# Two layers of a transformer on one core: attention's matrix order from a list schedule, its projections reordered

## What is computed

```
xn  = layernorm(x)                              # per token, no gain
q, k, v = split(xn @ w_qkv); 16 heads of 16     # 2 batches, 2048 tokens
q, k = rope(q), rope(k)
att = softmax(causal(q k^T / 4)); o = att @ v
x1  = x + o @ w_out + ffn(xn)                   # 256 -> 1024 -> 256, signed weights, gelu
```

## Time and profile before

| | us |
|---|---|
| profiled execution | 1663.91 |
| its span, first to last instruction | 1662.0 |
| projections, 0 to the first attention matmul | 148.7 |
| attention, 148.7 to the last copy | 871.3 |
| everything after | 642.0 |
| TensorE busy, share of the span | 1316.7, 79% |
| VectorE | 1271.5, 77% |
| ScalarE | 987.9, 59% |
| GpSimd | 319.4, 19% |

### The profile page before, as it was taken

The page is one execution under the profiler, slowest core; times in us unless marked ns, Lnnn a source line. Parts: engine busy times, 40 slices in busy tenths (PEclk is TensorE's granted clock), DMA queues, the critical chain, the costliest instruction groups (busy, mean ns, idle before and its releaser), DMA issues. The chain is left out here.

```text
span 1662.0 us, 27637 instructions
## 1 busy us (share of the span) xinstructions
PE 1316.7 (79%) x9558; PEld 588.4 (35%) x9558; DVE 1271.5 (77%) x1880; ACT 987.9 (59%) x1292; POOL 319.4 (19%) x574
## 2 busy tenths in 40 slices
PE   4783788888888888888888987888727876679987
PEld 2442222222222222222222222566523343358754
DVE  6984887988779787798897951478758999575668
ACT  3541355777768777677786886556417646236642
POOL 2210000110101101011010110322100047600365
PEclk9896577999889998899998998899967988789999
DMA  7875302140321403204032022656644134576767
GB/s 219 277 228 149 65 8 41 18 91 9 76 41 19 92 7 75 42 17 91 10 74 42 8 44 61 182 178 199 201 162 138 61 127 155 182 229 203 236 194 237
DMA packets 159723, 186.24 MB, mean 112 GB/s; under 512 B 19556, under 2 KB 135652, under 8 KB 158564
## 3 DMA queue, kind: packets, MB, share of 16 engines
q1 hardware_dynamic: 153448, 167.78, 35.9%
q0 software_dynamic: 6144, 16.79, 3.1%
HBM read 100.88 MB, written 83.36 MB: 111 GB/s over the span
## 5 line engine op out<-in xcount | busy, mean ns | idle before, releaser
L1270 ACT ACTIVATE att_prob<-att_score,late_score_scale 128x1024 f32<-128x1024 f32 (+3 forms) x640 | 594.7, 988 | 271.4 <-PE att_score L1359 269.3
L1241 DVE TENSOR_REDUCE att_m_part<-att_mx 128x2 f32<-128x1024 f32 (+3 forms) x408 | 473.3, 1160 | 97.5 <-PE att_mx L1308 43.6
L1343 PE MATMUL att_pv<-att_prob,early_v 128*32 128x512 f32 (+3 forms) x2560 | 324.5, 581 | 0.5 <-POOL att_prob L1206 0.2
L1302 PE MATMUL att_mx<-early_kop,early_qop 48*128 48x512 f16 (+3 forms) x944 | 181.1, 367 | 118.0 <-DVE att_m_part L1241 106.2
L1359 PE MATMUL att_score<-early_qop,early_kop 50*128 50x512 f16 (+3 forms) x1280 | 261.0, 369 | 12.4 <-ACT att_prob L1270 5.9
L1206 POOL TENSOR_SCALAR_AFFINE_SELECT att_prob<-att_prob 128x256 f32<-128x256 f32 x256 | 103.1, 407 | 767.6 <-ACT att_prob L1270 767.4
L1241 DVE TENSOR_REDUCE att_m_part<-att_mx_one 128x1 f32<-128x384 f32 (+1 forms) x336 | 220.9, 657 | 37.4 <-PE att_mx_one L1302 32.1
L1359 PEld LDWEIGHTS att_score<-early_qop,early_kop 50*128 50x128 f16 x1280 | 69.5, 95 | 293.5 <-ACT att_prob L1270 188.7
L1302 PE MATMUL att_mx_one<-early_kop,early_qop 48*128 48x384 f16 (+1 forms) x336 | 134.1, 399 | 19.7 <-DVE att_m_part L1241 15.9
L2108 PE MATMUL rwkv_prod<-rwkv_xm,late_mixT 128*128 128x512 f32 x192 | 100.1, 677 | 29.1 <-DVE rwkv_xm L1978 16.6
L1302 PEld LDWEIGHTS att_mx<-early_kop,early_qop 48*128 48x128 f16 x944 | 51.7, 97 | 190.9 <-DVE att_m_part L1241 165.9
(11 more groups left out here) (259 smaller groups left out, 1901.2 us busy)
## 6 DMA issues: line engine op xcount, KB each, us to landing
moe_xt<-rows SPq DMA_DIRECT2D x46, 256.0 KB, 3.3
results<-moe_y SPq DMA_DIRECT2D x46, 256.0 KB, 2.6
qk<-qkv_parts SPq DMA_DIRECT2D x32, 256.0 KB, 3.6
va<-qkv_v SPq DMA_DIRECT2D x8, 1024.0 KB, 6.5
early_v<-va SPq DMA_DIRECT2D x8, 1024.0 KB, 5.2
routing_xp<-parts SPq DMA_DIRECT2D x32, 256.0 KB, 3.7
rows<-att_zeros SPq DMA_DIRECT2D x8, 864.0 KB, 6.2
early_kop<-qk SPq DMA_DIRECT2D x48, 128.0 KB, 4.5
```

Source lines behind the costliest of these rows:

```text
L1241: nc.vector.tensor_reduce(cells[:, sides[0]:sides[-1] + 1, some], bank.rearrange("p a (h w) -> p a h w", w=w), AX.X, ALU.max).then_inc(m_f ...
L1270: nc.scalar.activation(prob[:, r % (PROBS * HP), :, n0:], score[:, r % 2, :, n0:], ACT.Exp, scale=late_weights.score_scale[:, 0:1])\
L1302: op = nc.tensor.matmul(bank[a][:, n * w:(n + 1) * w], qop[rows, slot, t, hp, i * P:(i + 1) * P], kop[rows, slot, hp, c * GT:c * GT + w], ...
L1343: op = nc.tensor.matmul(pv[at, n0:], v[:, slot, j, at], prob[:, (st * HP + h // 2) % (PROBS * HP), h % 2, n0:], start=(j == 0), stop=(j == ...
```

## The change

In the projections, from the second group on, `low` moves ahead of `products` on VectorE, `high` ahead of the late weight copies and `first_part` on ScalarE, and `ln.turn` ahead of `heads` on TensorE. The query loads of several blocks go in one DMA per head pair, part and side: 12 where 18 (or, for a whole head group, 24) were, and the semaphore targets follow; the first maxima of block 1 wait for all 12, those of block 2 for the values only.

In attention `spread_entries`, `spots` and `BEHIND` go. `matrix_order` writes one order over all head groups at build time. It keeps a clock for each engine and planned durations, and at each turn takes the maximum entry, score or value product that can start first; of equals the maximum first, then the score. The order of entries among themselves, of scores and of value products stays, as do their sizes and banks. ScalarE's exponentials and copies are taken from the same list: a copy stands where the list has the block's last value product. VectorE and GpSimd are unrolled.

```diff
     HP = HG // 2
     QB, KB = T // GT, T // P
     LOADS = 6
-    FIRST, REST = 16 * 2 * LOADS, 16 * (LOADS * (QB - 1) + 1)
+    FIRST, SECOND, REST = 16 * (LOADS + HP * LOADS), 16 * HP * LOADS, 16
 
     def __init__(self, s):
         self.qop = s.sb("qop", [P, 2, self.QB, self.HP, GT], F16)
@@ -643,12 +643,18 @@
                           qk_d[1, bass.ds(hg * (HG * D), HG * D), part, bass.ds(b * T, T)]
                           .rearrange("(hp a d) t -> a d hp t", a=2, d=D)[a]).then_inc(self.first_in[slot], 16)
 
-    def load_q(self, eng, qk_d, b, hg, slot, t, signal):
+    def load_q(self, eng, qk_d, b, hg, slot, blocks, signal):
+        n = blocks.stop - blocks.start
+        toks = bass.ds(b * T + blocks.start * GT, n * GT)
         for a, row, (_, part) in self.blocks:
             at = self.HALF * a + row * D
-            eng.dma_start(self.qop[at:at + D, slot, t],
-                          qk_d[0, bass.ds(hg * (HG * D), HG * D), part, bass.ds(b * T + t * GT, GT)]
-                          .rearrange("(hp a d) t -> a d hp t", a=2, d=D)[a]).then_inc(signal, 16)
+            src = qk_d[0, bass.ds(hg * (HG * D), HG * D), part, toks].rearrange("(hp a d) t -> a hp d t", a=2, d=D)[a]
+            if n == 1:
+                eng.dma_start(self.qop[at:at + D, slot, blocks.start], src.rearrange("hp d t -> d hp t")).then_inc(signal, 16)
+                continue
+            for hp in range(self.HP):
+                eng.dma_start(self.qop[at:at + D, slot, blocks, hp], src[hp].rearrange("d (q t) -> d q t", t=GT))\
+                    .then_inc(signal, 16)
 
     def load_v(self, eng, va_d, b, hg, slot):
         eng.dma_start(self.v[:, slot].rearrange("p j n -> p (j n)"),
@@ -769,12 +775,11 @@
                     if at[3][0] == G - 2:
...
                         att_in.load_k(sp, qk_d, 0, 0, 0)
-                        att_in.load_q(sp, qk_d, 0, 0, 0, 0, att_in.first_in[0])
+                        att_in.load_q(sp, qk_d, 0, 0, 0, slice(0, 1), att_in.first_in[0])
...
-            for t in range(1, att_in.QB):
-                att_in.load_q(sp, qk_d, 0, 0, 0, t, att_in.second_in if t == 1 else att_in.rest_in[0])
-            sp.sem_inc(att_in.rest_in[0], 16 * att_in.LOADS)
+            att_in.load_q(sp, qk_d, 0, 0, 0, slice(1, att_in.QB), att_in.second_in)
+            sp.sem_inc(att_in.first_in[0], att_in.FIRST - 16 * 2 * att_in.LOADS)
...
+                early = mid and mid[0] == 0
+                if new and not early:
+                    low(*new)
                 for p in range(QK):
                     if mid:
                         products(*mid, p)
                         rotated(*mid, p)
-                if new:
+                if new and early:
                     low(*new)
...
+                if new and not early:
+                    high(*new)
                 if mid and mid[0] >= late_from:
                     for n in late_turns(mid[0]):
                         late_weights.copy(nc, act, n, late_banks)
                 if mid:
                     first_part(*mid, 0)
-                if new:
+                if new and early:
                     high(*new)
...
+                if new and not early:
+                    ln.turn(nc, pe, new[0], new[1], ident[:, :])
                 if mid:
-                    if not mid[0]:
+                    if early:
                         pe.wait_ge(w.found, w.ready)
                     pe.wait_ge(ln.lo_done.sem, ln.lo_done.done(mid[0]))
                     heads(*mid, 0)
                     if mid[0] >= late_from:
                         late(mid[0])
                     heads(*mid, 1)
-                if new:
+                if new and early:
                     ln.turn(nc, pe, new[0], new[1], ident[:, :])
...
+    entries = [(0, e) for e in early if e != ("turn", LATE)]
+    for it in range(NIT):
+        entries += [(it, e) for e in late]
+        entries += [(it, e) if e == ("turn", LATE) else (it + 1, e) for e in early if it + 1 < NIT or e == ("turn", LATE)]
+    place = {entry: k for k, entry in enumerate(entries)}
+
+    def banks_of(k):
+        e = entries[k][1]
+        return (0, 1) if e[0] == "max" and len(e[5]) == 2 else (2,)
+    used, before = {}, []
+    for k in range(len(entries)):
+        before.append(max((used.get(bank, -1) for bank in banks_of(k)), default=-1))
+        used.update({bank: k for bank in banks_of(k)})
+
+    def columns(t, j):
+        return GT - max(0, j - TG * t) * P
+
+    def matrix_order():
+
+
+        hand, back, mask, row, copy = 250, 120, 420, 6500, 580
+        turn = {"max": 0, "score": 1, "value": 2}
+        score_at = [(it, st, hp) for it in range(NIT) for st in range(NS) for hp in range(HP)]
+        value_at = [(it, st) for it in range(NIT) for st in range(NS)]
+        pe = dve = act = pool = 0
+        exp_end, prob_end, value_end, out_end, found, rows = [], [], [], [], {}, {}
+        bank_end, order, done = [0] * BANKS, [], {"max": 0, "score": 0, "value": 0}
+        total = {"max": len(entries), "score": len(score_at), "value": len(value_at)}
+        while done != total:
+            ready = []
+            n = done["max"]
+            if n < total["max"]:
+                it, e = entries[n]
+                need = [bank_end[bank] for bank in banks_of(n)] + ([found[it, e[1]]] if e[0] == "turn" else [])
+                ready.append((max(need) + back, "max"))
+            n = done["score"]
+            if n < total["score"]:
+                it, st, hp = score_at[n]
+                if (it, steps[st][0]) in rows and n // HP < done["value"] + PROBS:
+                    need = [rows[it, steps[st][0]]] + [end + back for end in exp_end[n - 2:n - 1] if n >= 2]
+                    ready.append((max(need), "score"))
+            n = done["value"]
+            if (n + 1) * HP <= done["score"]:
+                need = prob_end[n * HP:(n + 1) * HP] + (out_end[-1:] if steps[n % NS][1] == 0 else [])
+                ready.append((max(need) + back, "value"))
+            when, kind = min((max(pe, when), turn[kind], kind) for when, kind in ready)[::2]
+            n = done[kind]
+            done[kind] += 1
+            if kind == "max":
+                it, e = entries[n]
+                if e[0] == "turn":
+                    pe = when + 270
+                    dve = max(dve, pe + hand) + 700
+                    rows[it, e[1]] = dve + row
+                else:
+                    size = len(e[3]) * width(e[1], e[2], e[4])
+                    pe = when + 20 + size * 5 // 12 + (60 * len(e[3]) if e[4] == e[1] else 0)
+                    dve = max(dve, pe + hand) + 70 + size * len(e[5]) * 100 // 96
+                    if e == chunks(e[1])[-1]:
+                        dve += 400
+                        found[it, e[1]] = dve
+                for bank in banks_of(n):
+                    bank_end[bank] = dve
+                order.append((kind, n))
+                continue
+            it, st = (score_at if kind == "score" else value_at)[n][:2]
+            t, j = steps[st]
+            if kind == "score":
+                pe = when + 20 + columns(t, j) * 5 // 12
+                start = max([act, pe + hand] + value_end[it * NS + st - PROBS:it * NS + st - PROBS + 1]
+                            if it * NS + st >= PROBS else [act, pe + hand])
+                act = start + 30 + columns(t, j) * 2 * 100 // 96
+                exp_end.append(act)
+                pool = max(pool, act + 100) + mask if j >= TG * t else pool
+                prob_end.append(pool if j >= TG * t else act)
+            else:
+                pe = when + 150 + columns(t, j) * 5 // 3
+                value_end.append(pe + hand)
+                if st in last_step:
+                    act = max(act, pe + hand) + copy
+                    out_end.append(act)
+            order.append((kind, it, st) + ((score_at[n][2],) if kind == "score" else ()))
+        return order
+
+    order = matrix_order()
...
+                att_in.load_q(sp, qk_d, b, hg, slot, slice(0, QB), first_in[slot])
...
+            for k, (it, e) in enumerate(entries):
+                entry(k, it, e)
...
+            for kind, it, st, *hp in [at for at in order if at[0] != "max"]:
+                if kind == "score":
+                    exps(it, st, *hp)
+                elif st in last_step:
+                    copy_out(it, steps[st][0])
...
+                if it > 0 and e == chunks(0)[0]:
+                    pe.wait_ge(first_in[slot], (it // 2 + 1) * FIRST)
+                    pe.wait_ge(rest_in[slot], (it // 2 + 1) * REST)
+                if it == 0 and e == chunks(1)[0]:
+                    pe.wait_ge(second_in, att_in.SECOND)
+                if it == 0 and e == chunks(2)[0]:
+                    pe.wait_ge(rest_in[0], REST)
+                if before[k] >= 0:
+                    pe.wait_ge(m_found, before[k] + 1)
...
+            for kind, *at in order:
+                if kind == "max":
+                    entry(*at)
```

(4 more changed lines are left out.)

227 lines of the change are left out of this document (64 added, 163 removed).

## The result

The changed kernel takes **1685.2 us** (median of four runs, 1683.4 to 1686.6) against 1665.1 for the kernel before in the same comparison (1660.1 to 1671.0): a ratio of **1.012 [1.010, 1.015]**, slower by a little over 1%. The prediction had 1605 us and faster. The profiled execution spans 1681.5 us, with a mean granted clock of 0.874 against 0.899.

The account below looks back on a forecast made before the run. VectorE, with the most work, sets the floor but waits for TensorE's badly ordered work. From 1663.9 us, -7 (projections and loads) - 10 (unrolling) - 28 (middle groups) - 13.4 (first group) = -58.4 gives 1605; range 1554 to 1668.

Parts of the forecast that it names:

- Query loads: End of projections, SyncE's queue: 12 loads in place of 18 at 0.589 us each save 3.5 us; ends 0 and 3.5.
- Unrolling: VectorE's attention loop: two jump stalls and the slower groups that begin there go, -10 us; ends -6 and -10.
- First group: Attention's first head group, 173.7 us: no idle at the first score, remainder at VectorE share 0.8875, -13.4 us; ends 0, -21.
- the list schedule in the middle groups: Six middle head groups: VectorE's busy share rises to 0.8875, 578.8 us against 607.1, -28 us; ends 0 and -70.
- full-width stretch: Trace from 500 to 520 us, VectorE busy 17.75 of 20 us (0.8875), the share used to price the middle groups.
- The last group: Last head group of attention: ScalarE's work bounds it, so 0 us is taken, -5 as the best.
- The copies: ScalarE's four block copies a group: added waits of 4.3 us at most, hidden within 25 us a group to spare.
- The projections' reorder: Projections: the next group's matmuls no longer start behind VectorE's low half, -3.5 of 5.9 us; ends 0 and 5.9.
- Value products in the way: Rival, middle groups: value products delay pair reductions, 0.5 us for each of 51 a group, 1706 us; chance 0.14.
- its own point of decision: Loss per VectorE pair reduction, 0.42 us, from which the whole kernel gets slower by over 1%.
- The clock: Rival, middle groups: TensorE waiting evenly in short pieces is granted less clock, 106.2 us each, 1677 in all; chance 0.06.

Follow-up runs that it names:

- old order: The changed kernel with the order of the kernel before in place of the list schedule, all else changed kept: 0.988 of the kernel before, 1642.4 us.
- the one try: The changed kernel with ScalarE's copies two exponentials later and TensorE's order kept: 1739 us, 1.047 of the kernel before.
- one number: The changed kernel with the planner's time for an exponential 16 hundredths longer: 1612.9 us, 0.970 of the kernel before.
- 12 hundredths: The changed kernel with the planner's time for an exponential 12 hundredths longer: 0.992 of the kernel before, middle groups 102.5 us.
- gap filled whole: The changed kernel with two unused extra matmuls behind every row-maxima entry of the stretch ahead of query block 3: 1.016 of the kernel before.
- old order with a late block 3: The old order kernel with block 3's row maxima spread over the first 22 steps of a head group instead of 18: 1.031 of the kernel before.

## Why the prediction was wrong

**Where it was right.** *Query loads:* 12 issues in 7.66 us where 18 took 10.60, 2.9 us less (predicted 3.5).

```profile
136.34 7.66 SPq L656 DMA_DIRECT2D early_qop<-qk  x12
```

*Unrolling:* a gain as forecast, but 15 us, beyond my end of 10; the stalls of the earlier trace rows are gone from the trace. I set the 2.9 us stalls against the 108 ns that the Trainium skill (Advanced Engine Details and Errata, Control Flow Timing) gives a compare-and-branch, and the trace's reading held. Another page of the Trainium skill (Runtime: NRT & Kernel Launch, Instruction fetch mechanics) says that a taken branch to code that was not fetched makes the engine wait for it; the stalls right at the jumps and the gain of unrolling agree, though no view here shows a fetch at those places. *First group:* against the old order with all else equal it fell by 15.4 us (170.8 to 155.4), predicted 13.4, and the idle of 3.5 us ahead of the first scores is gone. But the number is luck: the share that should have risen to 0.8875 fell, VectorE being busy 122.1 of 155.4 us (0.79) where it was 137.3 of 170.8 (0.80). The group is shorter because 15.2 us of VectorE's work moved out of it, and the last group has 16.0 us more of it.

**The step that failed** is the list schedule in the middle groups: "VectorE's share in its poor stretches should come up to that of the full-width stretch ... So I price all six groups at 0.8875", -28 us. Against the old order the six took 641.4 us where they had 603.8, **+37.6**, a share of 0.80. I had read the order's local quality (no standstill at a bank) and not where each block's rows come in it. Even the standstills at the banks did not go: from 210 to 900 us TensorE waits 75.9 us for the bank pair, 92.7 in the old order with all else equal. And the order lets the scores run ahead to the one place where they can't go on. The share of 0.886 is real, since planned exponentials 28 hundredths longer reach it, but by pacing, which the change left out and the order of before had.

**The last group** failed with it: "I take 0, and -5 as the best". It took 97.9 us, +17.4 against the old order's 80.5. VectorE had 54.8 us of work in it in place of 38.8: VectorE comes to this group 16 us of maxima behind the old order, whose places kept them a fixed number of steps ahead, and ScalarE waits 10.5 us for block 3's. I took a group bounded by ScalarE as out of the order's reach. The first and the last group together come to 253.3 us, 2.0 more than in the old order (251.3): what one gained the other lost. The three parts of the list schedule, -15.4 + 37.6 + 17.4, make +39.6, and the runs give +41. What these runs show is that the order costs this much and that its pace takes it away again; by which path it is paid, VectorE's queueing behind the wait or the low clock, stays open.

**The copies** were priced as hidden "as long as ScalarE keeps that slack". ScalarE's slack was not at hand where it was needed: behind the gap it is busy 33.0 of 37.2 us. Which share of the loss is theirs was not isolated; the one try moved the wait to TensorE.

**The projections' reorder**, -3.5, shows no gain that can be told from nothing: VectorE's wait for the matmuls fell from 5.9 to 2.0 us, and 3.8 of new waits for the high half took its place.

```profile
DVE qkv_ln_lo L352 <- ACT qkv_ln_hi L347: 3.8, 2, 2.6
...
DVE qkv_by_cos L828 <- PE qkv_qk_ps L102: 2.0, 2, 1.6
```

**The rivals.** "Value products in the way" named the right engine and the right loss (0.42 us for each of 51 pairs, its own point of decision), but as a mishap spread evenly. In the traces most of it sits behind the gap (9.3 us of idle time in a group where the old order has 4.7), and it is less when the plan is paced. "The clock" gave 106.2 us a group, 1677 in all, closest in number; its reason, short even waits, is not what was seen in the changed kernel, where the clock fell in the stretch of maxima alone. So it is in part luck that its number came closest; but the clock of 0.88 in the middle groups is what this rival named as its sign, and it is not refuted.

## What to carry to other kernels

In an order by earliest start, look for the operation with the longest chain behind it (here maxima of a whole block, a turn, row loads) and work out at which share of the fast consumer's work it is wanted and at which share of the slow producer's it is ready. If the consumer gets there first, the order has a stall, and the work held back by it comes afterwards all at once on the shared engine. Here a pace was worth more than the absence of small standstills (0.970 against 1.012 from one number; a due time for the chain was not tried), and the planner's own times showed the gap before anything ran. They did not show the whole cost: with 12 hundredths the gap was as long and the groups 4.4 us shorter. Moving a wait off one in-order engine is a gain only if nobody queues behind the one that gets it.

## What the runs showed of the hardware that was not expected

With two extra matmuls behind every entry (gap filled whole) TensorE was busy 3.1 to 3.8 us in the five-us stretches from 460 to 475 us, and the granted clock fell from 1.00 to 0.72 and 0.50 all the same, about as in the changed kernel with 2.2 to 2.4 us and none of them (0.91, 0.50, 0.50). Row loads took 3.9 us from the end of the row arithmetic (478.92 us) to the scores that waited for them (482.79) in the old order with a late block 3, four loads of 2.75 us of issue among it. Unrolling VectorE's and GpSimd's loops, where VectorE stood 2.95 and 2.89 us at its two jumps back, brought 15 us, more than the stalls themselves: the two groups that began with a jump came down from 106.3 and 106.0 us to 99.3 and 99.4.
